# Last layer's state-space stage: squares between two silus, their addition one unit later, mask tiles behind five output products

## The chip, the cores and the metric

The kernel is one program for one core of one Trainium2 chip. It computes a whole model of four layers in one launch. The metric is the device time of an execution in microseconds (us); smaller is better. The core has a matmul engine (TensorE, PE in the profile), a vector engine (VectorE, DVE), an activation engine (ScalarE, ACT), a general engine (GpSimd, POOL) and an engine that here only starts transfers (SyncE, SP). Each takes its instructions in the order of the program; they wait for one another through semaphores.

## The reference, cut to the stage that is changed

The change is in the last layer's attention, a state-space layer of 4096 inner columns (64 heads of 64). `hidden_states` is 1024 rows of 256. What matters:

```
z   = (hidden_states @ W_in)[..., :4096]
x   = silu(causal_conv1d((hidden_states @ W_in)[..., 4096:8192], conv_w, conv_b))
dt  = softplus(dt + dt_bias);  dtx = dt * x
L   = exp(where(mask, dA_cs[i] - dA_cs[j], -inf))        # per chunk of 128 rows, per head
Y   = einsum(C, B, L, dtx);  y = Y + D * x
yg  = y * silu(z)
rms = rsqrt(mean(yg * yg, over the 4096 columns) + 1e-5)
out = (yg * rms * norm_w) @ W_out
```

The mean of squares runs over all 4096 columns, so the squares of every part of `yg` are added up, and `rms` is applied once, at the end, to the summed products.

## The kernel before

`l3_attn` cuts the 4096 columns into N = 32 units of 128 columns (one pair of heads). Unit j is one call of each engine's `pair`; the units 0 to 3 are written out, the units 4 to 31 run in a loop of two units per pass (`passes`). Columns lie on the partitions, the 1024 rows along the free dimension in two halves of 512, or eight blocks of 128. s = j % 2 chooses the buffer.

**TensorE in unit j** (line 2803 on). First the output products of unit j-3 (`output`, L2797): eight products, each `yg` block by `wo`, summed over all units into four PSUM banks. Each stands in the trace as two records of 128x256. In the midst of them stands `free_for_differences`, which waits until VectorE has read what lies in the banks 4 to 7 (semaphores xt_read and y_read); it is put right before the last product of the part that it is given. Then `differences`: sixteen small mask tiles (L2764, which write the large negative numbers of the mask) and four matmuls (L2769) that put dA_cs[i] - dA_cs[j] into the banks 4 to 7. Then the other output products. Then 24 projection matmuls (L2827), which give x and z halves; y of unit j-1 (`make_y`, L2784, 32 records), whose halves wait for ScalarE's silu of z; and the transposes of x (L2839), one group of four per half, whose halves wait for ScalarE's silu of x.

**ScalarE in unit j** (line 2922 on): four exponentials (L2913) of the differences; `squares` (L2920), which writes the squares of yg of unit j-2 into `ysq`, the one buffer of them; two evacuations of x (L2658, the first tap of the convolution); a table load (L2944); silu of z half 0 (L2950), silu of x half 0 (L2952), silu of z half 1, silu of x half 1; a table load (L2955). A silu of x waits for the convolution of its half on VectorE.

**VectorE in unit j**: `weigh` (L3032), four multiplications of 128x512 with both inputs in SBUF, called n0 to n3 below, each behind its exponential; six convolution taps (L2662), three per half, with one input in PSUM; `skip` (L3045), two; the two multiplications by dt (L3080), which free the transposes' banks and raise xt_read; `gate` (L3054), two, both inputs in SBUF.

**GpSimd in unit j**: in every other unit `steps` (L3122, L3124); the two halves of the weights' split (L3147, L3150), small copies (L3156, L3159); `scale_output` (L3136), which scales `wo` for unit j-1 and waits until the output products of unit j-3 are done; waits for its own last results and a semaphore to SyncE (L3168), upon which SyncE fetches weights; `add_squares` (L3129), 128x1024, sqsum += ysq, both inputs in SBUF, for unit j-2.

`ysq` is written by `squares` and read by `add_squares`: the squares of one unit wait (sq_added) until those of the unit before it have been added. At the end TensorE sums sqsum over the partitions (L2856), which waits for the last addition.

Of the kernel before, what the change touches and what calls it, by code (L numbers as in the profile page):

```python
# [2584 lines left out]
def l3_attn(k):  # L2585
# [11 lines left out]
    with Stage(k, "L3a", k.now) as st:  # L2597
# [81 lines left out]
        def early(j, n=2):  # L2679

            return isinstance(j, int) and j < n

        ln = Norm(k, st)
        with nc.Block() as block:
# [14 lines left out]
            def _(pe):  # L2699
# [89 lines left out]
                def output(pe, j, o, half, part=range(4), of_next=None):  # L2789

                    pe.wait_ge(S["wo_ready"], j + 1)
                    pe.wait_ge(S["y_ready"], j * 2 + half + 1)
                    for b in part:
                        g = 4 * half + b
                        if b == part[-1] and of_next is not None:
                            free_for_differences(pe, *of_next)
                        mm = nc.tensor.matmul(ps[g // 2][:, (g % 2) * C:(g % 2 + 1) * C],  # L2797
                                              yg[:, o, g * P:(g + 1) * P], wo[:, o, :], start=False, stop=False,
                                              skip_group_check=True)
                    if half == 1 and part[-1] == 3:  # L2800
                        mm.then_inc(S["out_done"], 1)

                def pair(pe, j, s, i):
                    first = is_first(j)
                    if is_second(j):
                        clear_sums(pe)
                    if not early(j, 3):
                        output(pe, j - 3, 1 - s, 0)
                        output(pe, j - 3, 1 - s, 1, (0, 1), (j, i))
                    elif not first:  # L2810
                        free_for_differences(pe, j, i)
                    if not first:
                        differences(pe, s)
                    if not early(j, 3):
                        output(pe, j - 3, 1 - s, 1, (2, 3))
                    if first:
                        make_cs(pe)
                    pe.wait_ge(S["w_split"], j + 1)
                    for at_d, (name, wm, sem) in enumerate((("x", wx[s], "x_psum"), ("z", wz[s], "z_psum"))):
                        for half in range(2):  # L2820
                            if first:
                                pe.wait_ge(S["bc_conv"], at_d + 1)
                            else:
                                pe.wait_ge(S["diff_read"], j * 4 + 2 * at_d + half + 1)
                            for kc in range(KC):
                                for at, (a, b) in enumerate(THREE):
                                    mm = nc.tensor.matmul(bank(name, half)[:, :], wm[a][:, kc, :],  # L2827
                                                          (xh, xl)[b][:, kc, half * HALF:(half + 1) * HALF],
                                                          start=(kc + at == 0), stop=(kc + at == KC + 1))
                            mm.then_inc(S[sem], 1)  # L2830
                    if first:
                        make_cb(pe)
                    else:
                        make_y(pe, j, 1 - s)
                    for half in range(2):
                        pe.wait_ge(S["x_ready"], j * 2 + half + 1)
                        for b in range(4):
                            g = 4 * half + b
                            mm = nc.tensor.transpose(bank("t", half)[:, b * P:(b + 1) * P],  # L2839
                                                     xT[:, s, g * P:(g + 1) * P], k.ident)  # L2840
                        mm.then_inc(S["xt_psum"], 1)
                    if first:
                        free_for_differences(pe, j, i)
                        differences(pe, s)
# [21 lines left out]
            def _(act):  # L2866
# [55 lines left out]
                def pair(act, j, s, i):  # L2922
                    first = is_first(j)
                    if not first:
                        exponents(act, j, s)
                    if not early(j):
                        squares(act, j - 2, s)
                    act.wait_ge(s_load[s], i * 16 + 16)
                    if first:
                        sums(0)  # L2930
                        sums(1)
                    if early(j):
                        act.wait_ge(S["bc_ready"], j + 1)
                    for half in range(2):
                        act.wait_ge(S["x_psum"], j * 2 + half + 1)
                        conv_first(act, bank("x", half)[:, :],
                                   conv[:, s, 4 * half:4 * half + 4, :].rearrange("p b t -> p (b t)"),
                                   taps[s][:, 3:4], cb[s]).then_inc(S["x_scaled"], 1)
                    if first:
                        bc_silu(1, cT)  # L2940
                        sums(2)
                        sums(3)
                    else:
                        nc.scalar.preload_act_table(ACT.Silu)  # L2944
                    for half in range(2):
                        t = slice(half * HALF, (half + 1) * HALF)
                        act.wait_ge(S["z_psum"], j * 2 + half + 1)
                        if not early(j):
                            act.wait_ge(S["y_ready"], j * 2 - 2)
                        nc.scalar.activation(sz[:, s, t], bank("z", half)[:, :], ACT.Silu).then_inc(S["z_read"], 1)  # L2950
                        act.wait_ge(S["x_conv"], j * 2 + half + 1)
                        nc.scalar.activation(xT[:, s, t],  # L2952
                                             conv[:, s, 4 * half:4 * half + 4, :].rearrange("p b t -> p (b t)"),
                                             ACT.Silu).then_inc(S["x_ready"], 1)
                    nc.scalar.preload_act_table(ACT.Exp)  # L2955
                    if first:
                        exponents(act, j, s)
# [148 lines left out]
            def _(pool):  # L3106
# [32 lines left out]
                def pair(pool, j, s, i):  # L3139

                    if not early(j) and s == 0:
                        steps(pool, i)
                    pool.wait_ge(s_load[s], i * 16 + 16)
                    if not early(j):
                        pool.wait_ge(S["z_psum"], j * 2 - 2)
                    w2 = slot[s][:, 0:2 * KC * P]
                    nc.gpsimd.tensor_tensor(wh[:, s, :], w2, k.c["zero"].to_broadcast([P, 2 * KC * P]),  # L3147
                                            ALU.add).then_inc(S["w_high"], 1)
                    pool.wait_ge(S["w_high"], j + 1)
                    nc.gpsimd.tensor_tensor(wl[:, s, :], w2, wh[:, s, :].bitcast(F32),  # L3150
                                            ALU.subtract).then_inc(S["w_split"], 1)

                    if not early(j):
                        pool.wait_ge(S["xt_read"], j * 2 - 2)
                    hs = slice(j * 2, j * 2 + 2) if isinstance(j, int) else bass.ds(j * 2, 2)
                    nc.gpsimd.tensor_copy(dtc[:, s, :, :], dt[:, :, hs]).then_inc(S["pair_small"], 1)  # L3156
                    if not early(j):
                        pool.wait_ge(S["y_read"], j * 2 - 2)
                    nc.gpsimd.tensor_tensor(dcols[:, s, :], dcol[s], k.c["zero"], ALU.add).then_inc(S["d_ready"], 1)  # L3159
                    if is_second(j):  # L3160
                        steps(pool, 0)
                    if not is_first(j):
                        scale_output(pool, j - 1, 1 - s)
                        pool.wait_ge(S["x_ready"], j * 2)
                        pool.wait_ge(S["w_split"], j)
                        pool.wait_ge(S["wo_ready"], j)
                        pool.wait_ge(S["d_ready"], j)
                        pool.sem_inc(S["slot_read"], 2)  # L3168
                    if not early(j):
                        add_squares(pool, j - 2)  # L3170

                def tail(pool):
                    scale_output(pool, N - 1, 1)
                    add_squares(pool, N - 2)
                    add_squares(pool, N - 1)

# [745 lines left out]
```

## Time and profile before

| what | value |
|---|---|
| median of 3 runs | 1874.9 us (1874.17 to 1876.9) |
| profiled execution, its own time | 1872.17 us |
| its span in the trace | 1870.0 us |
| PE busy | 1655.7 us (89%) |
| DVE busy | 1175.1 us (63%) |
| ACT busy | 931.7 us (50%) |
| POOL busy | 461.8 us (25%) |
| units 3 to 31 of the stage | about 1126 to 1527 us of the span, 13.5 or 13.7 us each |

Busy shares are averages over all stages of the model. A row of the timeline gives the start in the span, the duration in us, the engine, line and operation, the tiles written and read, and in brackets the idle time of the engine ahead of it with what ended it. For a merged row (x4) the duration runs from the first start to the last end. The modelled ends of PE records overlap with the next starts, so PE is read by its starts.

### The profile page before, as it was taken

The numbers are of one execution on the slowest core, as the hardware profiler recorded it, in microseconds if no ns is written. First come the engines' busy times: TensorE is split into PE (matmuls) and PEld (weight loads), VectorE is DVE, ScalarE is ACT, GpSimd is POOL, SyncE is SP. The second block draws the span as 40 slices with busy tenths as digits, with TensorE's granted clock in tenths as the row PEclk, the third lists the DMA queues.
The fourth block names the chain that finished last, engine by engine and source line by source line (L and its number), as shares of the span: only waits on it lengthen the run. The fifth ranks groups of instructions, "written<-read, shape, count | busy, mean of one in ns | idle before, by whom it ended". The sixth has DMA issues, their size and how long they took to land. (4 is left out here: it accounts for less than half of the span.)

```text
span 1870.0 us, 38238 instructions
## 1 busy us (share of the span) xinstructions
PE 1655.7 (89%) x14220; PEld 1276.5 (68%) x14220; DVE 1175.1 (63%) x2316; ACT 931.7 (50%) x1979; POOL 461.8 (25%) x510
## 2 busy tenths in 40 slices
PE   7988856789999889996688869999999987999898
PEld 4767733558888745663477747777777766888687
DVE  4676688556666622224665588888888875666642
ACT  2455567236656521121255456676766644555552
POOL 2030021023333131221400225454454531000220
PEclk9999978799999999998799889999999998999999
DMA  2020000300000092222000100010101003111000
GB/s 103 3 94 3 4 30 31 117 18 27 26 25 25 18 371 45 47 35 67 14 2 3 50 18 27 26 34 26 34 26 33 27 9 126 35 34 34 1 1 24
DMA packets 27684, 77.91 MB, mean 42 GB/s; under 512 B 2993, under 2 KB 14897, under 8 KB 25393
## 3 DMA queue, kind: packets, MB, share of 16 engines
q1 hardware_dynamic: 23488, 71.19, 11.1%
q0 software_dynamic: 4080, 5.13, 1.7%
q8 instruction: 79, 1.29, 0.3%
q14 instruction: 37, 0.30, 0.1%
HBM read 63.03 MB, written 13.28 MB: 41 GB/s over the span
## 5 line engine op out<-in xcount | busy, mean ns | idle before, releaser
L2662 DVE SCALAR_TENSOR_TENSOR arena<-bank,arena 128x508 f32<-128x508 f32 (+2 forms) x204 | 151.5, 743 | 18.4 <-DVE arena L2662 6.6
L3032 DVE TENSOR_TENSOR L3a_decays<-L3a_decays,L3a_cb_masked 128x512 f32<-128x512 f32 x128 | 94.8, 799 | 49.5 <-ACT L3a_decays L2913 49.5
L2797 PE MATMUL bank<-L3a_wo,L3a_y_gated 128*128 128x256 f32 x512 | 125.0, 388 | 0.0
L2913 ACT ACTIVATE L3a_decays<-bank 128x512 f32<-128x512 f32 x128 | 66.1, 604 | 103.3 <-PE bank L2769 103.3
L2827 PE MATMUL bank<-L3a_xnT_high,L3a_w_high 128*128 128x512 f32 x256 | 105.1, 410 | 1.5 <-ACT L3a_decays L2913 1.5
L2797 PEld LDWEIGHTS bank<-L3a_wo,L3a_y_gated 128*128 128x128 f32 x512 | 91.2, 190 | 21.0 <-issue 11.4
L228 PE MATMUL bank<-const 128*128 128x512 f32 (+1 forms) x154 | 73.7, 619 | 33.7 <-PEq L66 33.7
L2827 PE MATMUL bank<-L3a_xnT_high,L3a_w_low 128*128 128x512 f32 x256 | 100.5, 392 | 0.0
L2827 PE MATMUL bank<-L3a_xnT_low,L3a_w_high 128*128 128x512 f32 x256 | 100.2, 391 | 0.0
L3129 POOL TENSOR_TENSOR arena<-arena 128x1024 f32<-128x1024 f32 x32 | 86.3, 2695 | 44.4 <-ACT arena L2920 44.4
L2064 ACT ACTIVATE arena<-bank 128x512 f32<-128x512 f32 x23 | 13.7, 597 | 145.4 <-PE bank L2013 145.4
L2013 PE MATMUL bank<-L1f_experts,xnT 128*128 x184 | 85.0, 606 | 0.8 <-DVE xnT L2116 0.6
L228 PEld LDWEIGHTS bank<-const 128*128 128x128 f32 x154 | 29.2, 201 | 65.6 <-issue 65.4
L827 ACT ACTIVATE L1x_p<-bank,L1x_minus_max,L1x_q_scale 128x128 f32<-128x128 f32 x128 | 56.6, 452 | 32.0 <-DVE L1x_minus_max L1861 32.0
L2784 PE MATMUL bank<-L3a_decays,L3a_dtx 128*64 128x128 f32 x1024 | 67.2, 279 | 3.9 <-ACT arena L2950 2.1
L2784 PEld LDWEIGHTS bank<-L3a_decays,L3a_dtx 128*64 128x64 f32 x1024 | 54.8, 136 | 22.0 <-ACT arena L2950 17.9
L827 ACT ACTIVATE L3x_p<-L3x_masked_scores,L3x_minus_max 128x128 f32<-128x128 f32 x128 | 49.7, 389 | 38.8 <-DVE L3x_minus_max L3368 38.8
L2110 DVE TENSOR_TENSOR L1f_hidden<-arena,bank 128x512 f32<-128x512 f32 x23 | 15.8, 688 | 82.5 <-PE bank L2013 82.5
L1974 POOL DMA_INDIRECT rows_added<-L1f_y,L1f_token x23 | 35.7, 1554 | 114.9 <-DVE L1f_y L2129 111.8
L1689 POOL TENSOR_TENSOR L1x_q_squares<-L1x_qT 128x512 f32<-128x512 f32 x32 | 36.6, 1161 | 101.6 <-ACT L1x_qT L1802 101.6
L672 POOL TENSOR_TENSOR x<-x,arena 128x256 f32<-128x256 f32 x48 | 34.6, 756 | 109.3 <-ACT xn L215 96.4
L2952 ACT ACTIVATE L3a_xT<-arena 128x512 f32<-128x512 f32 x64 | 40.2, 628 | 37.8 <-DVEq L3070 37.8
(643 smaller groups left out, 4654.5 us busy)
## 6 DMA issues: line engine op xcount, KB each, us to landing
arena<-in_L3p SPq DMA_DIRECT2D x32, 388.0 KB, 3.0
L1f_experts<-in_L1f SPq DMA_DIRECT2D x8, 1536.0 KB, 18.9
arena<-in_L1x SPq DMA_DIRECT2D x18, 384.0 KB, 3.0
arena<-in_L3x SPq DMA_DIRECT2D x18, 384.0 KB, 3.0
arena<-in_L0f SPq DMA_DIRECT2D x1, 4224.0 KB, 12.9
arena<-in_L3f SPq DMA_DIRECT2D x1, 4055.0 KB, 12.8
rows_sent<-L1a_blank SPq DMA_DIRECT2D x1, 2967.0 KB, 13.6
xnT<-rows_sent SPq DMA_DIRECT2D x23, 129.0 KB, 2.0
```

The costliest lines, as they stand in the source:

```text
L228: self.nc.tensor.matmul(self.k.ps[bank][:, 0:width], self.k.ident, self.k.const[:, 0:width], start=True, stop=True)
L827: ins = nc.scalar.activation(self.p[:, h, b * P:(b + 1) * P], src[:, b * P:(b + 1) * P], ACT.Exp, bias=self.nb[:, h, b:b + 1], scale=scale ...
L1689: nc.gpsimd.tensor_tensor(sq[:, h * HALF:(h + 1) * HALF], q, q, ALU.mult).then_inc(s_sq, 1)
L2013: mm = nc.tensor.matmul(ps[2 * (t % 2) + m][:, :], rowsT[:, t % 2, kc, :], experts[:, bass.ds(first + (m * KC + kc) * I, I)], start=(kc == 0),
L2662: return nc.vector.scalar_tensor_tensor(dst[:, :, d:], psum[:, :, 0:P - d], wcol, dst[:, :, d:], ALU.mult, ALU.add)
L2784: mm = nc.tensor.matmul(bank("y", half)[h * HD:(h + 1) * HD, b * P:(b + 1) * P], dtx[:, o, g, h, :], dec[:, o, h, g, :], start=True, stop= ...
L2797: mm = nc.tensor.matmul(ps[g // 2][:, (g % 2) * C:(g % 2 + 1) * C], yg[:, o, g * P:(g + 1) * P], wo[:, o, :], start=False, stop=False, ski ...
L2827: mm = nc.tensor.matmul(bank(name, half)[:, :], wm[a][:, kc, :], (xh, xl)[b][:, kc, half * HALF:(half + 1) * HALF], start=(kc + at == 0), ...
L2913: nc.scalar.activation(d4[:, n * HALF:(n + 1) * HALF], bank("d", n)[:, :], ACT.Exp).then_inc(S["diff_read"], 1)
L2952: nc.scalar.activation(xT[:, s, t], conv[:, s, 4 * half:4 * half + 4, :].rearrange("p b t -> p (b t)"), ACT.Silu).then_inc(S["x_ready"], 1)
L3032: nc.vector.tensor_tensor(d, d, cbm[:, 4 * half:4 * half + 4, :].rearrange("p b t -> p (b t)"), ALU.mult).then_inc(S["dec_ready"], 1)
L3129: nc.gpsimd.tensor_tensor(sqsum, sqsum, ysq, ALU.add).then_inc(S["sq_added"], 1)
```

## The change

Three things, all in `l3_attn`. `squares(act, j - 2, s)` no longer stands behind the exponentials, but behind the silu of z half 1, ahead of the silu of x half 1. `add_squares` in unit j adds the squares of unit j-3, not j-2, and the end has three additions instead of two. The output products of TensorE are split five and three around the mask tiles and differences, where they were split six and two; the wait of `free_for_differences` moves with them and stands ahead of the fifth product.

```diff
                         output(pe, j - 3, 1 - s, 0)
-                        output(pe, j - 3, 1 - s, 1, (0, 1), (j, i))
+                        output(pe, j - 3, 1 - s, 1, (0,), (j, i))
                     if not first:
                         differences(pe, s)
                     if not early(j, 3):
-                        output(pe, j - 3, 1 - s, 1, (2, 3))
+                        output(pe, j - 3, 1 - s, 1, (1, 2, 3))
...
                         exponents(act, j, s)
-                    if not early(j):
-                        squares(act, j - 2, s)
                     act.wait_ge(s_load[s], i * 16 + 16)
...
                         nc.scalar.activation(sz[:, s, t], bank("z", half)[:, :], ACT.Silu).then_inc(S["z_read"], 1)
+                        if half == 1 and not early(j):
+                            squares(act, j - 2, s)
                         act.wait_ge(S["x_conv"], j * 2 + half + 1)
...
                         pool.sem_inc(S["slot_read"], 2)
-                    if not early(j):
-                        add_squares(pool, j - 2)
+                    if not early(j, 3):
+                        add_squares(pool, j - 3)
...
                 def tail(pool):
                     scale_output(pool, N - 1, 1)
+                    add_squares(pool, N - 3)
                     add_squares(pool, N - 2)
                     add_squares(pool, N - 1)
```

On ScalarE, in the loop's unit, from the last exponential (L2913) to the silu of x half 1 (L2952); this is the piece of the difference, in which unmarked rows stand in both kernels and lines from 2926 on are shifted:

```order
 L2913 ACTIVATE L3a_decays<-bank 128x512
+L2926 ISA
+L2933 REGISTER_ALU
+L2658 ACTIVATE arena<-bank,arena 128x512
+L2933 REGISTER_ALU
+L2658 ACTIVATE arena<-bank,arena 128x512
+L2942 ACT_TABLE_LOAD
+L2948 ACTIVATE arena<-bank 128x512
+L2952 ACTIVATE L3a_xT<-arena 128x512
+L2948 ACTIVATE arena<-bank 128x512
 L2918 ISA
 L2919 REGISTER_ALU
 L2920 ACTIVATE arena<-L3a_y_gated 128x1024
```

The squares (L2920) moved from ahead of the two evacuations (L2658) to behind the second silu of z; the number of table loads stays two per unit.

On GpSimd, in the first unit of the loop's pass, from the scaling of `wo` (L3136) on, before:

```order
L3136 TENSOR_TENSOR L3a_wo<-arena 128x256
L3129 TENSOR_TENSOR arena<-arena 128x1024
L3145 ISA
L3147 TENSOR_TENSOR L3a_w_high<-arena,const 128x512
L3149 REGISTER_ALU
L3150 TENSOR_TENSOR L3a_w_low<-arena,L3a_w_high 128x512
```

and after:

```order
L3136 TENSOR_TENSOR L3a_wo<-arena 128x256
L3128 REGISTER_ALU
L3129 TENSOR_TENSOR arena<-arena 128x1024
L3145 ISA
L3147 TENSOR_TENSOR L3a_w_high<-arena,const 128x512
L3149 REGISTER_ALU
```

The addition (L3129) keeps its place behind the scaling; what moved is the squares that it waits for: those of the unit before, not of the unit running on ScalarE.

## Rows read from the trace of the kernel before

**Rows 1.** Busy time by engine over 26 units, with granted clock (PEclk)
```profile
core 0: us, PE busy (x) PEld busy (x) DVE busy (x) ACT busy (x) POOL busy (x), PEclk, DMA share, GB/s
1150.00:1500.00 350.00, 344.65 (x2590) 261.74 (x2588) 287.91 (x414) 237.88 (x335) 173.84 (x181) 1.00 0.10 29
```
**Rows 2.** Timeline of PE, one unit; columns as told above
```profile
1308.27 0.42 PE L2764 MATMUL bank<-L3a_later_tiles,L3a_ident 32*32 32x128 bf16 x16
...
1318.56 0.66 PE L2839 MATMUL bank<-const,L3a_xT 128*128 128x128 f32 x4 [0.16 <-ACT L3a_xT L2952]
1319.05 2.77 PE L2797 MATMUL bank<-L3a_wo,L3a_y_gated 128*128 128x256 f32 x12
1321.75 0.42 PE L2764 MATMUL bank<-L3a_later_tiles,L3a_ident 32*32 32x128 bf16 x16
...
1322.54 1.13 PE L2797 MATMUL bank<-L3a_wo,L3a_y_gated 128*128 128x256 f32 x4
```
**Rows 3.** Timeline of ACT, the same unit
```profile
1311.16 1.08 ACT L2920 ACTIVATE arena<-L3a_y_gated 128x1024 f32<-128x1024 f32 x1
1312.11 1.64 ACT L2658 ACTIVATE arena<-bank,arena 128x512 f32<-128x512 f32 x2
1313.76 1.28 ACT L2944 ACT_TABLE_LOAD   x1
...
1316.07 0.59 ACT L2950 ACTIVATE arena<-bank 128x512 f32<-128x512 f32 x1
1317.87 0.63 ACT L2952 ACTIVATE L3a_xT<-arena 128x512 f32<-128x512 f32 x1 [1.21 <-DVEq L3070]
```
**Rows 4.** Timeline of DVE, the same unit
```profile
1309.86 2.92 DVE L3032 TENSOR_TENSOR L3a_decays<-L3a_decays,L3a_cb_masked 128x512 f32<-128x512 f32 x4 [1.58 <-ACT L3a_decays L2913]
1312.94 2.30 DVE L2662 SCALAR_TENSOR_TENSOR arena<-bank,arena 128x508 f32<-128x508 f32 x3 [0.16 <-ACT arena L2658]
1315.48 2.30 DVE L2662 SCALAR_TENSOR_TENSOR arena<-bank,arena 128x508 f32<-128x508 f32 x3 [0.24 <-DVE arena L2662]
...
1319.52 1.28 DVE L3080 TENSOR_TENSOR L3a_dtx<-bank,L3a_dt_pair 128x512 f32<-128x512 f32 x2
```
**Rows 5.** Timeline of POOL, the same unit
```profile
1310.27 0.76 POOL L3136 TENSOR_TENSOR L3a_wo<-arena 128x256 f32<-128x256 f32 x1 [4.12 <-PE bank L2797]
1312.32 2.73 POOL L3129 TENSOR_TENSOR arena<-arena 128x1024 f32<-128x1024 f32 x1 [1.29 <-ACT arena L2920]
```
**Rows 6.** Timeline of DVE, single records of the same unit's weighing, n1 and n3
```profile
1310.47 1.10 DVE L3032 TENSOR_TENSOR L3a_decays<-L3a_decays,L3a_cb_masked 128x512 f32<-128x512 f32 x1
1312.10 0.68 DVE L3032 TENSOR_TENSOR L3a_decays<-L3a_decays,L3a_cb_masked 128x512 f32<-128x512 f32 x1
```
**Rows 7.** Timeline of unit 1, DVE and POOL, then one undisturbed POOL record of later
```profile
1105.52 1.53 DVE L3032 TENSOR_TENSOR L3a_decays<-L3a_decays,L3a_cb_masked 128x512 f32<-128x512 f32 x1
1106.46 1.48 POOL L3147 TENSOR_TENSOR L3a_w_high<-arena,const 128x512 fp32r<-128x512 f32 x1
1106.97 1.52 DVE L3032 TENSOR_TENSOR L3a_decays<-L3a_decays,L3a_cb_masked 128x512 f32<-128x512 f32 x1
1108.02 1.43 POOL L3150 TENSOR_TENSOR L3a_w_low<-arena,L3a_w_high 128x512 fp32r<-128x512 f32 x1
...
1140.83 1.04 POOL L3147 TENSOR_TENSOR L3a_w_high<-arena,const 128x512 fp32r<-128x512 f32 x1
```
**Rows 8.** Timeline of the stage's end: POOL, DVE, POOL, PE
```profile
1526.30 0.61 POOL L3136 TENSOR_TENSOR L3a_wo<-arena 128x256 f32<-128x256 f32 x1 [7.70 <-PE bank L2797]
1526.87 2.37 POOL L3129 TENSOR_TENSOR arena<-arena 128x1024 f32<-128x1024 f32 x1
...
1528.82 0.96 DVE L3054 TENSOR_TENSOR L3a_y_gated<-L3a_y_gated,arena 128x512 f32<-128x512 f32 x1
...
1531.61 2.35 POOL L3129 TENSOR_TENSOR arena<-arena 128x1024 f32<-128x1024 f32 x1 [2.38 <-ACT arena L2920]
...
1535.05 1.84 PE L2856 MATMUL bank<-const,arena 128*128 128x1 f32 x16
```
**Rows 9.** Busy time and granted clock in four 2 us stretches, units 1 and 2
```profile
1115.00:1117.00 2.00, 0.90 (x7) 0.42 (x5) 2.00 (x4) 1.66 (x2) 0.63 (x2) 1.00 0.00 0
1117.00:1119.00 2.00, 0.87 (x20) 0.36 (x20) 1.68 (x3) 0.41 (x1) 0.12 (x1) 0.96 0.35 71
1119.00:1121.00 2.00, 1.67 (x4) 1.41 (x5) 1.78 (x3) 2.00 (x5) 0.00 (x0) 0.50 0.33 132
1121.00:1123.00 2.00, 2.00 (x7) 1.57 (x7) 0.71 (x2) 1.27 (x2) 1.33 (x1) 0.69 0.00 0
```

## What the change will do to the time

> **What bounds the kernel now.** I read the busy time by stretch first. Over 26 units of the stage PE is busy 344.65 of 350 us at full clock, VectorE 287.91 [rows 1]. So the matmul engine looks like the bound, with 2% left. The timelines of one unit say what that 2% is, and that a second bound is just as near. Let T be the start of the mask tiles (1308.27 in the unit shown). The next tiles start at 1321.75, so this unit is 13.48 us long [rows 2]. A loop through four engines closes in exactly that time: tiles, exponentials, weighing from T+1.59, first tap at T+4.67, last tap done at T+9.51, silu of x half 1 at T+9.60 [rows 3, 4], second transposes at T+10.29, for which PE waits, output products at T+10.78, and after twelve records of them (six products) the next tiles at T+13.48 [rows 2]. Twelve records take 2.70 us, one product 0.45 us. The loop shows an idle PE ahead of the second transposes; hence both what shortens this loop and what lengthens it counts.
>
> The second view is VectorE against GpSimd. The weighing takes 2.92 us [rows 4], though n3 alone is 0.68 long; n1 is 1.10 long [rows 6]. GpSimd's scaling L3136 came at 1310.27, in the midst of n0, and ended at 1311.03; n1 ended at 1311.57, 0.54 later [rows 5, 6]. In unit 1 the two engines alternate: L3147 starts at 1106.46 and lasts 1.48, where it needs 1.04 undisturbed; n2, recorded from 1106.97, ends at 1108.49, 0.55 after L3147's end; L3150, which came during that, ends at 1109.45 [rows 7]. So a multiplication of VectorE with two SBUF inputs and such an instruction of GpSimd never run side by side: whoever comes while the other runs waits for all of it, and one that has waited goes before the other's next. The disputed instruction itself shows it twice. L3129 needs 2.37 undisturbed [rows 8] but 2.73 when it came at 1312.32 while n3 was running [rows 5]: it ended at 1315.05, so it ran from 1312.68, about 0.1 before n3's recorded end of 1312.78. At the stage's end a `gate` that came under L3129 lasted 0.96 and ended 0.54 after it [rows 8]. The taps, one input in PSUM, keep 2.30 us for three under a running L3129 [rows 4, 5].
>
> **The products.** With five products ahead of the tiles, 0.45 us goes out of the loop, and three follow. PE's own work is unchanged. Everything tied to the tiles (exponentials, weighing) starts 0.45 earlier against the end of the output products, and so against L3136, which waits for them. L3136 now comes at T+2.00 [rows 2, 5]; it will come at T+2.45.
>
> **The squares.** Their place behind the exponentials costs 0.95 us of ScalarE (start to next start), but the evacuations behind them wait for PE's projections anyway: VectorE idles only 0.16 for the first [rows 3, 4]. In the new place they fill 0.95 of a 1.21 us wait: silu of z half 1 at 1316.07, squares 0.5 later, silu of x half 1 could start at 1317.52, before it is wanted at 1317.87 [rows 3]. No table load is added. So alone this costs nothing and gives back up to 0.16.
>
> **The addition, one unit later.** This is the part that decides. Now L3129 waits 1.29 us behind L3136 for the squares [rows 5], and comes at T+4.05, when only the tail of n3 is left. After the change its squares were made a unit ago, so it comes right behind L3136. Between the two stand only satisfied waits and one semaphore; where nothing stands between, the next starts as the first ends (1526.87 against 1526.30 + 0.61) [rows 8]. I take 0.25 us for them, an estimate with bounds of 0 and 0.5 worked from this row and from the 0.13 that GpSimd's small instructions keep between them.
>
> Now the order on the shared resource. n0 from T+1.59; n1 recorded from T+2.20, runs until T+2.88 and lets go at T+2.75 (0.13 before its end, since L3136 must have begun at 1310.42 to be through at 1311.03, and n0 of 0.68 would be recorded to 1310.54). L3136 comes at T+2.45, inside n1, and runs T+2.75 to T+3.36 (0.61 undisturbed [rows 8]). n2 follows, ends at T+3.90, lets go at T+3.77. L3129 comes at T+3.36 + 0.25 = T+3.61, while n2 runs, so it is next: T+3.77 to T+6.14. n3 must wait and ends 0.54 later, at T+6.68 instead of T+4.51. The taps start at T+6.61 (a follower starts 0.07 before the recorded end) instead of T+4.67: **1.94 us later**. Nothing hides it: the last tap, the silu of x half 1, the second transposes and the output products are the loop. The wait ahead of the fifth product needs L3080, which ends at T+12.53 now [rows 4] and at T+14.47 then, while the fifth product's weights would load at about T+14.4: bounds 0 and 0.3, I take 0.10. Per unit: -0.45 + 1.94 + 0.10 = **+1.59 us**.
>
> The Trainium skill, SBUF — State Buffer, section "Who interferes with whom", says that a VectorE instruction with two SBUF inputs contends with a GpSimd instruction that reads SBUF, and that the loser fully blocks; by a shared bandwidth the sum would be the third rival below, by the lock it is this one, and the traces of unit 1 agree with the lock. The skill's Perfetto Trace Analysis, section "GPSIMD Engine Instruction", warns that GpSimd's recorded spans are unreliable and start-to-start spacing should be used; by spacing, L3147 to L3150 in unit 1 is 1.56 us and the alternation stays, so the sum would stay too.
>
> **The ends.** Additions run in the units 3 to 31, 29 of them. The tiles of unit 3 come 0.45 earlier; 28 intervals follow, 28 x 1.59 = 44.5; unit 31's transposes are late by 1.94 with no tiles behind. At the end of the stage three additions stand in a row. Now the last one ends at 1533.96 and L2856 starts at 1535.05 [rows 8]. The first (2.37) frees `ysq` at about 1529.3, squares take 1.06, the second addition ends near 1532.8, squares again, the third near 1536.3: L2856 starts near 1536.4, **+1.35**. Sum: 44.5 - 0.45 + 1.94 + 1.35 = 47.3 us. The profiled execution took 1872.17 (span 1870.0); that gives 1919.5, and since its time is 2.7 under the median of 1874.9, **1922.2** for the median. Own range by per-unit bounds of 1.3 to 2.0 (the tiles' wait, and 0.2 either way for reading starts): 1914 to 1934.
>
> **Rivals.** (1) *L3129 misses n2.* If it comes more than 0.41 us behind L3136's end, n2 has let go and n3 holds on; the addition then waits and disturbs only taps, which it doesn't slow. Then the weighing ends near T+4.5, the taps start near T+4.6, and the squares in their new place bound the silu, at 9.25 of the old count (1317.52): 0.35 less per unit, 29 x 0.35 = 10.2, less 1.35 at the end: 1866.1, faster. For it: the margin is only 0.16, and GpSimd's starts are the least certain. Against it: 0.04 of overlap in rows 8, and four plain waits would have to cost over 0.1 each. (2) *Sharing.* If VectorE only ran at half pace under L3129, n3 would end near T+5.5: taps +0.78, per unit -0.45 + 0.78 + 0.05 = 0.38, 28 of them 10.6, with ends of -0.45 + 0.78 + 1.35 12.3, hence 1887.2. Rows 7 speak against. (3) *The clock.* PE will idle some 2 us per unit, 1.3 of it in one piece (silu of z half 1 stands behind silu of x half 0 on ScalarE, which waits for the late taps). After unit 1, with PE busy 0.9 of 2 us for several stretches, the granted clock fell to 0.50, the 1.2 GHz level, and 2 us went at that level [rows 9]. Were that so once in each unit, another 1 us per unit would be lost, 1950.2. Against it: between the gaps PE is busy over 5 us on end.
>
> **How the numbers follow.** Forecast 0.80, rival 1 0.12, rival 2 0.04, rival 3 0.04. The forecast's own range holds most of its 0.80 (0.76); from 1886 it takes in rival 2, up to 1945 the thinner part of rival 3: 0.81 or so. Rival 1 alone is on the faster side: faster by over 0.2% (3.7 us, about what a measurement of this kernel can tell from no change) 0.12, within it 0.01, slower 0.87.
>
> **What would show it.** In the profile after: the four L3032 of a unit together 5.1 us rather than 2.92, one of them near 2.9 (in rows 7 the longest is 1.53); L3129 starting 0.1 to 0.4 behind L3136's end, and lasting about 2.5; L3136 near 0.9; the first tap with no wait for ScalarE; PE waiting for the silu of z half 1 (L2784) and longer for the silu of x half 1 (L2839); units of 15.1 us; a mean clock of 1.00. A longest L3032 near 1.1 and L3129 behind n3 would mean rival 1; all four L3032 stretched alike would mean rival 2. What makes the prediction wrong is the one number 0.25, against its threshold of 0.41.

## The result and the profile after

| | before | after |
|---|---|---|
| median | 1874.54 us (4 runs) | 1933.29 us (4 runs, 1927.40 to 1933.57) |
| ratio | 1 | 1.0298, interval 1.0282 to 1.0314 |
| span of the profiled execution | 1870.0 us | 1931.6 us |
| mean of the 28 unit intervals from unit 3's to unit 31's tiles | 13.56 us | 15.40 us |

The change makes the kernel 3% slower. The forecast was 1922.2 in a range of 1886 to 1945. The direction and the mechanism hold; the size was 11 us short.

The row of busy times by stretch, over the same 350 us as [rows 1]: PE is idle 39.5 us of 350 where it was idle 5.4, and the granted clock is still 1.00.

```profile
1150.00:1500.00 350.00, 310.48 (x2276) 230.72 (x2276) 301.94 (x362) 215.79 (x297) 153.09 (x159) 1.00 0.09 26
```

The timeline of VectorE in one unit (T = 1304.40), the answer to [rows 4, 6]: first the weighing as a whole, then its single records n0 to n3, then the two groups of taps and L3080.

```profile
1306.00 5.13 DVE L3032 TENSOR_TENSOR L3a_decays<-L3a_decays,L3a_cb_masked 128x512 f32<-128x512 f32 x4 [1.35 <-ACT L3a_decays L2913]
...
1306.00 0.69 DVE L3032 TENSOR_TENSOR L3a_decays<-L3a_decays,L3a_cb_masked 128x512 f32<-128x512 f32 x1 [1.35 <-ACT L3a_decays L2913]
...
1306.61 0.69 DVE L3032 TENSOR_TENSOR L3a_decays<-L3a_decays,L3a_cb_masked 128x512 f32<-128x512 f32 x1
...
1307.21 1.10 DVE L3032 TENSOR_TENSOR L3a_decays<-L3a_decays,L3a_cb_masked 128x512 f32<-128x512 f32 x1
...
1308.24 2.89 DVE L3032 TENSOR_TENSOR L3a_decays<-L3a_decays,L3a_cb_masked 128x512 f32<-128x512 f32 x1
...
1311.05 2.29 DVE L2662 SCALAR_TENSOR_TENSOR arena<-bank,arena 128x508 f32<-128x508 f32 x3
1313.57 2.30 DVE L2662 SCALAR_TENSOR_TENSOR arena<-bank,arena 128x508 f32<-128x508 f32 x3 [0.24 <-DVE arena L2662]
...
1317.61 1.28 DVE L3080 TENSOR_TENSOR L3a_dtx<-bank,L3a_dt_pair 128x512 f32<-128x512 f32 x2
```

The timeline of GpSimd in the same unit, the answer to [rows 5]:

```profile
1306.84 0.92 POOL L3136 TENSOR_TENSOR L3a_wo<-arena 128x256 f32<-128x256 f32 x1 [4.32 <-PE bank L2797]
1308.08 2.49 POOL L3129 TENSOR_TENSOR arena<-arena 128x1024 f32<-128x1024 f32 x1 [0.32 <-issue]
```

Read the two together, with T = 1304.40, the start of the mask tiles. L3136 comes at 1306.84 inside n1 and ends at 1307.76. n2, kept back by it, ends at 1308.31, 0.55 later. L3129 comes at 1308.08, 0.32 behind L3136, while n2 runs. It ends at 1310.57. n3, recorded from 1308.24, ends at 1311.13, 0.56 behind L3129's end. So n3 has waited for all of the addition: 2.89 us instead of 0.68. The first tap starts at T+6.65; before it was T+4.67. In the other of the two kinds of unit in the loop L3129 comes 0.25 behind L3136, and the weighing takes 5.12.

The timeline of PE in the same unit, up to the next unit's tiles, the answer to [rows 2]:

```profile
1314.59 1.09 PE L2784 MATMUL bank<-L3a_decays,L3a_dtx 128*64 128x128 f32 x16 [1.19 <-ACT arena L2948]
1315.62 0.66 PE L2839 MATMUL bank<-const,L3a_xT 128*128 128x128 f32 x4
1316.64 0.66 PE L2839 MATMUL bank<-const,L3a_xT 128*128 128x128 f32 x4 [0.37 <-ACT L3a_xT L2952]
1317.14 1.89 PE L2797 MATMUL bank<-L3a_wo,L3a_y_gated 128*128 128x256 f32 x8
1319.25 0.69 PE L2797 MATMUL bank<-L3a_wo,L3a_y_gated 128*128 128x256 f32 x2 [0.22 <-issue]
1319.87 0.42 PE L2764 MATMUL bank<-L3a_later_tiles,L3a_ident 32*32 32x128 bf16 x16
```

The second half of y waits 1.19 us for the silu of z, the second transposes wait for the silu of x, and the fifth product (the x2 row) stands apart from the four ahead of it. L3080, which its wait is for, ends at 1318.89; the tiles start at 1319.87, 0.98 later. In the other 27 of the 28 intervals it is 0.95 or 0.96.

ScalarE, the answer to [rows 3]: the squares fill part of the wait for the convolution, and the silu of x half 1 still waits 0.48 us for VectorE behind them. The squares hold nobody up.

```profile
1314.44 1.05 ACT L2920 ACTIVATE arena<-L3a_y_gated 128x1024 f32<-128x1024 f32 x1
1315.96 0.63 ACT L2952 ACTIVATE L3a_xT<-arena 128x512 f32<-128x512 f32 x1 [0.48 <-DVEq L3070]
```

### The profile page after: what moved, and what is told of

Read it like the earlier page. It is cut to its first block and busy times, and to the rows that moved or that the text cites. A ratio compares the mean times of both kernels' runs of the same rounds, so it can differ in the third digit from the quotient of the medians.

```text
span 1931.6 us, 38263 instructions
## 1 busy us (share of the span) xinstructions
PE 1670.3 (86%) x14216; PEld 1280.0 (66%) x14220; DVE 1236.8 (64%) x2316; ACT 938.0 (49%) x1979; POOL 461.5 (24%) x510
## 5 line engine op out<-in xcount | busy, mean ns | idle before, releaser
L3032 DVE TENSOR_TENSOR L3a_decays<-L3a_decays,L3a_cb_masked 128x512 f32<-128x512 f32 x128 | 159.7, 1308 | 45.9 <-ACT L3a_decays L2913 45.9
L2797 PE MATMUL bank<-L3a_wo,L3a_y_gated 128*128 128x256 f32 x512 | 131.1, 393 | 2.8 <-issue 2.7
L2913 ACT ACTIVATE L3a_decays<-bank 128x512 f32<-128x512 f32 x128 | 66.2, 605 | 99.3 <-PE bank L2769 99.3
L3129 POOL TENSOR_TENSOR arena<-arena 128x1024 f32<-128x1024 f32 x32 | 80.3, 2508 | 10.9 <-issue 8.3
L2658 ACT ACTIVATE arena<-bank,arena 128x512 f32<-128x512 f32 x68 | 52.9, 780 | 43.5 <-PE bank L2827 43.5
L228 PEld LDWEIGHTS bank<-const 128*128 128x128 f32 x154 | 29.6, 204 | 65.2 <-issue 65.1
L2952 ACT ACTIVATE L3a_xT<-arena 128x512 f32<-128x512 f32 x64 | 40.4, 631 | 51.0 <-DVEq L3070 51.0
L3136 POOL TENSOR_TENSOR L3a_wo<-arena 128x256 f32<-128x256 f32 x32 | 28.8, 901 | 135.7 <-PE bank L2797 135.7
## 6 DMA issues: line engine op xcount, KB each, us to landing
L1f_experts<-in_L1f SPq DMA_DIRECT2D x8, 1536.0 KB, 14.3
```

What stands on the lines that cost most here:

```text
L228: self.nc.tensor.matmul(self.k.ps[bank][:, 0:width], self.k.ident, self.k.const[:, 0:width], start=True, stop=True)
L2658: return nc.scalar.activation(dst, psum, ACT.Identity, bias=bias, scale=w3)
L2913: nc.scalar.activation(d4[:, n * HALF:(n + 1) * HALF], bank("d", n)[:, :], ACT.Exp).then_inc(S["diff_read"], 1)
L2952: nc.scalar.activation(xT[:, s, t], conv[:, s, 4 * half:4 * half + 4, :].rearrange("p b t -> p (b t)"), ACT.Silu).then_inc(S["x_ready"], 1)
L3032: nc.vector.tensor_tensor(d, d, cbm[:, 4 * half:4 * half + 4, :].rearrange("p b t -> p (b t)"), ALU.mult).then_inc(S["dec_ready"], 1)
L3129: nc.gpsimd.tensor_tensor(sqsum, sqsum, ysq, ALU.add).then_inc(S["sq_added"], 1)
```

## The experiments

Each unit interval below is the mean of the 28 intervals from unit 3's to unit 31's tiles in the profiled execution. It is a better witness than the total, because stages that no experiment touches differ by up to 4 us between executions: from L2856 to the end of the span it is 335.0 us in the kernel before and 339.2 in f_wait_gate_behind. The kernels a to d were timed on one chip beside the kernel before (there 1876.49 us), i, h, f and g on another (1873.39), k and e on a third (1876.81). So kernels of different groups are compared by their ratios and unit intervals.

| kernel | unit interval | total, median | ratio to before, interval |
|---|---|---|---|
| a_wait_weigh | 13.37 | 1869.77 | 0.9967 (0.9956 to 0.9979) |
| b_six_two | 15.73 | 1941.05 | 1.0341 (1.0321 to 1.0362) |
| c_half_add | 14.29 | 1895.50 | 1.0099 (1.0075 to 1.0122) |
| d_split_only | 13.44 | 1866.94 | 0.9955 (0.9939 to 0.9972) |
| i_gate_behind | 15.07 | 1921.46 | 1.0255 (1.0225 to 1.0284) |
| h_split_gate_behind | 13.16 | 1862.34 | 0.9939 (0.9923 to 0.9955) |
| f_wait_gate_behind | 13.20 | 1865.41 | 0.9955 (0.9941 to 0.9969) |
| g_squares_only | 15.25 | 1918.60 | 1.0241 (1.0203 to 1.0279) |
| k_wait_third | 13.36 | 1869.56 | 0.9959 (0.9945 to 0.9973) |
| e_wait_six_two | 13.32 | 1868.32 | 0.9961 (0.9943 to 0.9979) |

**a_wait_weigh: the addition behind the weighing.** Against the changed kernel:

```diff
                     if not early(j, 3):
+                        pool.wait_ge(S["dec_ready"], j * 4 + 4)
                         add_squares(pool, j - 3)
```

> The changed kernel, in which GpSimd's addition L3129 also waits until VectorE's fourth multiplication n3 of the same unit is done. Nothing else is moved. Theory 1 (exclusive turns: n3 had to wait for all of L3129): n3 is 0.68 us long again, the weighing about 2.9 us, the first tap starts near T+4.6 (T = start of the mask tiles), units of 13.3 to 13.6 us, total 1868 to 1878. Rival A (the loss is from the squares between two silus delaying the silu of x half 1): the addition's place is innocent, units stay at 15.4 us, total near 1930. Rival B (the loss is from the split five and three, with its earlier wait): the same, near 1930.

One added wait takes the unit from 15.40 to 13.37 us and the total from 1933 to 1870. GpSimd's addition and the whole weighing of one unit, from this kernel's timelines:

```profile
1308.07 2.40 POOL L3129 TENSOR_TENSOR arena<-arena 128x1024 f32<-128x1024 f32 x1 [1.31 <-DVE L3a_decays L3032]
...
1305.00 2.92 DVE L3032 TENSOR_TENSOR L3a_decays<-L3a_decays,L3a_cb_masked 128x512 f32<-128x512 f32 x4 [1.35 <-ACT L3a_decays L2913]
1308.00 2.30 DVE L2662 SCALAR_TENSOR_TENSOR arena<-bank,arena 128x508 f32<-128x508 f32 x3
```

The addition lasts 2.40, near its undisturbed 2.37, beside taps that keep 2.30, and the weighing is 2.92 again. Squares and split stand as in the changed kernel, so the rivals A and B, by which one of them was the loss, are out. The order of the two engines' instructions was the loss; with that order mended, the changed kernel is no longer slower than the one before.

**c_half_add: the price against the length of the addition.** This kernel leaves half of the squares out of the sum.

```diff
-                    nc.gpsimd.tensor_tensor(sqsum, sqsum, ysq, ALU.add).then_inc(S["sq_added"], 1)
+                    nc.gpsimd.tensor_tensor(sqsum[:, 0:HALF], sqsum[:, 0:HALF], ysq[:, 0:HALF], ALU.add).then_inc(S["sq_added"], 1)
```

> The changed kernel in which every addition L3129 adds only the first 512 of 1024 columns; the other half of the squares is left out of the sum. It lasts about 1.2 us instead of 2.37. Theory 1 (n3 waits for the whole instruction): the longest L3032 falls from 2.89 to about 1.7 us, units fall from 15.41 by 1.18 to about 14.2, total 1933 - 28 x 1.18 - 2 = about 1897. Rival C (VectorE runs at a part of its pace under GpSimd): the weighing shrinks by half as much, units near 14.8, total near 1915.

The unit falls by 1.11 us to 14.29, the total to 1895.5. In this kernel's timelines n3 is 1.77 long, ends at 1306.30, and the addition ends at 1305.75:

```profile
1304.31 1.44 POOL L3129 TENSOR_TENSOR arena<-arena 128x512 f32<-128x512 f32 x1 [0.26 <-issue]
...
1304.53 1.77 DVE L3032 TENSOR_TENSOR L3a_decays<-L3a_decays,L3a_cb_masked 128x512 f32<-128x512 f32 x1
```

n3 ends 0.55 or 0.56 behind the addition whether that is long or short. So it waits for the whole instruction; sharing at a part of the pace (rival C, 1915) would have halved the difference.

**k_wait_third: who comes first.** As a_wait_weigh, with j * 4 + 3 in place of j * 4 + 4.

> The changed kernel, in which the addition waits for VectorE's third multiplication n2, not for the fourth. Theory 1 (whoever comes first has the turn, and for all of it): the semaphore of n2 lets L3129 come about 0.1 us after n2's end, when n3, recorded from 0.07 before n2's end, has already begun; so n3 stays 0.68 long, L3129 waits for it (2.7 us long), and the units are the 13.37 us of the kernel that waits for n3; total 1866 to 1874. This also tests the forecast's threshold: 0.41 us after L3136's end. Rival (GpSimd always wins, or the two share): n3 is lengthened by 1 to 2.4 us and the total is 1895 to 1933.

The addition now comes at 1309.15 behind n2. n3 has been recorded from 1308.92, keeps its 0.68, and the addition is the one that waits (2.72 instead of 2.40):

```profile
1309.15 2.72 POOL L3129 TENSOR_TENSOR arena<-arena 128x1024 f32<-128x1024 f32 x1 [0.71 <-DVE L3a_decays L3032]
...
1308.92 0.68 DVE L3032 TENSOR_TENSOR L3a_decays<-L3a_decays,L3a_cb_masked 128x512 f32<-128x512 f32 x1
```

L3136 ends at 1308.45 here, so the addition came 0.70 behind it. In the changed kernel it came 0.32 behind it and in this case cost 2 us a unit. The threshold of 0.41 lies between the two; it was not approached closer.

**b_six_two: the changed kernel with the old split.**

```diff
-                        output(pe, j - 3, 1 - s, 1, (0,), (j, i))
+                        output(pe, j - 3, 1 - s, 1, (0, 1), (j, i))
...
-                        output(pe, j - 3, 1 - s, 1, (1, 2, 3))
+                        output(pe, j - 3, 1 - s, 1, (2, 3))
```

> The changed kernel with the output products split six and two again, as before; squares and additions stay as changed. Theory 1: L3136 now comes in n0, L3129 in n1, so n2 (not n3) waits for all of L3129 and lasts near 2.9 us; the weighing ends near T+6.7 all the same, the wait ahead of the sixth product costs nothing, and units take 13.56 + 1.94 = 15.5 us: total 1925 to 1935. Rival B (the split is the cause): back to about 1875.

The split is not the cause: without it the kernel is slower still, by a ratio of 1.0341 where the changed kernel has 1.0298. It is also 6 us above the 1925 to 1935 that were expected. Here it is n2 that lasts 2.89, as expected, since L3136 and L3129 come one multiplication earlier. Most units take 15.44 to 15.66, where 15.5 was expected, but 6 of 28 take 16.45. Busy times over one unit that stays short (the first two rows) and one that doesn't (the other three) show what differs; the columns are those of [rows 1]:

```profile
1298.00:1301.00 3.00, 1.30 (x19) 0.89 (x18) 2.66 (x5) 1.39 (x4) 2.92 (x3) 1.00 0.00 0
1301.00:1303.00 2.00, 1.65 (x20) 1.24 (x20) 1.62 (x3) 1.51 (x3) 0.28 (x2) 1.00 0.00 0
...
1313.50:1316.50 3.00, 1.38 (x18) 0.85 (x16) 2.66 (x5) 1.39 (x4) 1.74 (x3) 1.00 0.00 0
1316.50:1318.50 2.00, 1.92 (x17) 1.59 (x18) 1.55 (x3) 1.52 (x3) 0.00 (x0) 0.56 0.00 0
1318.50:1320.50 2.00, 2.00 (x10) 1.97 (x11) 1.94 (x4) 1.36 (x2) 0.19 (x1) 0.59 0.00 0
```

PE has been idle for 1.63 us between the two halves of y, and then the granted clock falls to the 1.2 GHz level for some 3 us. Six such units, each 0.8 to 1.0 us longer, make up about the 6 us above what was expected (an estimate from the intervals). This is rival 3 of the prediction. But a gap of that length doesn't decide it alone: the unit of the first two rows has a gap of 1.64 us, every one of the 28 has one of 1.62 us or more, and the clock falls in only six. In the changed kernel, with gaps of 1.2, the clock stayed at 1.00 over the 350 us above.

**d_split_only: the split alone, on the kernel before.** The diff is the reverse of the one above.

> The kernel before, with only the output products split five and three; squares and additions as before. Theory 1 with the wait ahead of the fifth product costing 0.10 us, as predicted: L3129 still comes at T+4.05 behind n2, units shorter by 0.45 - 0.10, but no less than PE's own work of about 13.1, total near 1865. With that wait costing 0.40 us, as the changed kernel's trace suggests: units shorter by 0.05 only, total 1872 to 1876. In both the weighing stays at 2.9 us.

13.44 us a unit, 1866.9 in all: 0.45% faster than before. The gain of 0.12 us a unit lies between the two expectations. In all 28 intervals the tiles follow 0.95 to 0.99 behind L3080's end, here from 1315.05 to 1316.01:

```profile
1313.77 1.28 DVE L3080 TENSOR_TENSOR L3a_dtx<-bank,L3a_dt_pair 128x512 f32<-128x512 f32 x2
...
1316.01 0.42 PE L2764 MATMUL bank<-L3a_later_tiles,L3a_ident 32*32 32x128 bf16 x16
```

So part of the split's 0.45 us is lost to the wait ahead of the fifth product, here too.

**i_gate_behind: the waits for the banks behind the fifth product.** The changed kernel with:

```diff
                     for b in part:
                         g = 4 * half + b
-                        if b == part[-1] and of_next is not None:
-                            free_for_differences(pe, *of_next)
                         mm = nc.tensor.matmul(...)
+                    if of_next is not None:
+                        free_for_differences(pe, *of_next)
+                        pe.sem_inc(S["tiles_free"], 1)
```

(`tiles_free` is a new semaphore that nobody waits for; it only stands between the waits and the mask tile.)

> The changed kernel, with TensorE's waits for the banks (free_for_differences) put behind the fifth output product instead of ahead of it. Theory 1, with the part of the prediction that was too small named: in the changed kernel the tiles start 0.97 us behind the end of L3080 in every unit, because the fifth product starts only after the wait; the loop closes over L3080 and not over the second transposes. With the wait behind the product the tiles start at T + 12.74 + 2.25 = T+15.0 to 15.1, units 15.4 -> 15.05, total about 10 us under the changed kernel's 1933: 1920 to 1926. The weighing stays at 5.1 us. Rival (the extra 11 us over the forecast are from elsewhere, such as the clock): units stay at 15.4, total 1930 to 1934.

1921.46 us, 15.07 a unit. The products now run through, ten records in 2.26 us, and the tiles start with 0.51 behind L3080's end (1314.40 to 1314.91) instead of 0.98:

```profile
1312.65 2.32 PE L2795 MATMUL bank<-L3a_wo,L3a_y_gated 128*128 128x256 f32 x10
1314.91 0.42 PE L2764 MATMUL bank<-L3a_later_tiles,L3a_ident 32*32 32x128 bf16 x16
```

**h_split_gate_behind: the kernel before, split and waits moved, nothing else.** d_split_only with the diff of i_gate_behind.

> The kernel before, with the products split five and three and the waits for the banks behind the fifth product. Theory 1: without this the split alone gives units of 13.45 us with the tiles 0.96 behind the end of L3080; now the tiles start when the fifth product is through, output products at T+10.85, tiles at T+13.1: units 13.1 to 13.25 us, which is TensorE's own work; total about 28 x 0.27 = 8 us under the split alone's 1867: 1857 to 1863. Rival: TensorE's work bounds at 13.45 already: no change against the split alone.

13.16 us a unit, 1862.34 in all, 0.61% faster than before: the shortest unit and the lowest time of the kernels tried, though its interval overlaps with those of f, d, k and e. PE is busy 338.27 of 340 us, so little but PE's own work is left in the stage:

```profile
1150.00:1490.00 340.00, 338.27 (x2592) 264.96 (x2591) 288.64 (x414) 239.11 (x337) 177.48 (x182) 1.00 0.09 29
```

**f_wait_gate_behind: all of the change, both amendments.** a_wait_weigh with the diff of i_gate_behind.

> The changed kernel with both amendments: the addition waits for the fourth multiplication, and the waits for the banks stand behind the fifth product. Theory 1: units from 13.37 to 13.1 or 13.2 us, total 1862 to 1866, 1 to 3 us over the same without moved squares, for the three additions in a row at the stage's end cost 1.5 us or so.

13.20 us, 1865.41. The changed kernel can be had 0.45% faster than before with the two amendments, but h_split_gate_behind, which leaves squares and additions alone, is no slower. From the last tiles to L2856 the three additions in a row cost 1.5 us (24.8 against 23.3).

**g_squares_only: the squares alone, the addition left behind them in the same unit.** The ScalarE part of the change's diff on the kernel before.

> The kernel before, with only the squares moved between the two silus; the addition stays in the same unit and so waits for them. Theory 1: the squares cost ScalarE nothing, but the addition runs near T+9.4 to T+11.8, and GpSimd's queue behind it (steps, weights' split) is then late for TensorE in every second unit by 0.5 to 1.3 us: total 1882 to 1897. Rival (squares in that place delay the silu of x half 1 itself): ScalarE's row of the silu starts later than its convolution is done, in every unit.

Expected up to 1897, measured 1918.6: the direction was right, the price was too small. Units alternate between 14.7 and 15.9. The rival accounts for very little: ScalarE's silu of x half 1 starts at 1310.01, 0.24 behind the end of its taps (1309.77), where it was 0.09 in the kernel before (1317.78 to 1317.87), so the squares hold it by 0.15 us at most. GpSimd's queue is the first part of the loss. The addition waits for the squares until 1323.67; behind it stand the next unit's steps, the last of which ends at 1328.77, and the sixth output product waits for them:

```profile
1323.67 2.36 POOL L3129 TENSOR_TENSOR arena<-arena 128x1024 f32<-128x1024 f32 x1 [5.66 <-ACT arena L2920]
1326.54 0.78 POOL L3122 TENSOR_TENSOR L3a_diff_left<-L3a_cs_left,const 128x256 fp32r<-128x256 f32 x1 [0.50 <-POOL arena L3129]
1327.29 1.48 POOL L3124 TENSOR_TENSOR L3a_diff_right<-xn,const 128x512 fp32r<-128x512 f32 x1
...
1329.19 0.69 PE L2797 MATMUL bank<-L3a_wo,L3a_y_gated 128*128 128x256 f32 x2 [2.02 <-POOL L3a_diff_right L3124]
```

L3124 itself is 1.48 here instead of 1.04, because it now meets VectorE's `gate`.

The second part of the loss is the clock. Behind that gap of 2 us ahead of the sixth product the granted clock falls to the 1.2 GHz level:

```profile
1295.50:1298.50 3.00, 1.04 (x5) 0.57 (x3) 1.73 (x3) 0.00 (x0) 2.59 (x3) 1.00 0.00 0
1298.50:1302.50 4.00, 3.94 (x27) 2.55 (x28) 1.46 (x3) 2.07 (x4) 2.12 (x5) 0.64 0.00 0
```

There are 14 such gaps in the loop, one in every second unit, and the clock falls behind 13 of them, all but the first. The unit behind the first takes 13.21 us, those behind the others 14.61 to 14.76. So the clock costs about 13 x 1.48 = 19 us (an estimate from these intervals), most of the 21.6 us by which the time lies above the upper end of what was expected.

With the squares in their new place the addition must therefore move too, if it isn't to hold up the steps behind it, and where it moves to was the question of this case.

**e_wait_six_two: squares and addition moved, the addition behind the weighing, the old split.**

> The changed kernel with the addition behind the fourth multiplication, as before, and the output products split six and two again: only the squares' new place and the later addition are left of the change. Theory 1: the first tap no longer waits 0.16 us for ScalarE, the loop over the second transposes shortens by that, units 13.40 instead of 13.57, the three additions at the end cost 1.35 us: total 1870 to 1874 against 1874 before. Rival (squares in front of the silu of x half 1 delay it): units of 13.6 or more, total 1875 to 1880.

13.32 us a unit, 0.24 less than before, and 1868.3 in all. The first tap follows the weighing without the 0.16 us wait; with T = 1302.93 it starts at T+4.43, where it was T+4.67:

```profile
1304.52 2.92 DVE L3032 TENSOR_TENSOR L3a_decays<-L3a_decays,L3a_cb_masked 128x512 f32<-128x512 f32 x4 [1.59 <-ACT L3a_decays L2913]
1307.36 2.29 DVE L2662 SCALAR_TENSOR_TENSOR arena<-bank,arena 128x508 f32<-128x508 f32 x3
```

So the squares' new place is worth a little, as the prediction said, and somewhat more than its 0.16, since a follower also starts 0.07 to 0.08 ahead of the recorded end. The rival is out.

## Why the prediction was right, and what was too small

**What bounds the kernel.** Right. The loop through tiles, weighing, taps, silu, transposes and output products exists, and both ways of shortening it (d_split_only, e_wait_six_two) shorten the unit.

**The order on the shared resource.** Right, within 0.07 us. Foretold: L3136 at T+2.45, n2's end T+3.90, L3129 at T+3.61, n3's end T+6.68, first tap T+6.61. Measured: T+2.44, T+3.91, T+3.68, T+6.73, T+6.65. The number on which all hung, L3129's distance behind L3136's end, was 0.32 in this kind of unit and 0.25 in the other, under the 0.41 of the threshold. It had been an estimate with bounds of 0 and 0.5, which reach beyond the threshold, so that it fell on the foretold side was in part luck. c_half_add and k_wait_third show the rule apart from this kernel's timing.

**The squares cost nothing by themselves.** Right as to ScalarE (the silu of x half 1 still waits for the convolution behind them), and e_wait_six_two has the gain. But "alone this costs nothing" holds only of ScalarE: with the addition left in the same unit, g_squares_only is 2.4% slower.

**The wait ahead of the fifth product: 0.10 us a unit, bounds 0 and 0.3.** This is the term that was mis-sized, and its measured value lies just outside its bounds. Over the 28 intervals the unit grew by 15.40 - 13.56 = 1.84 instead of 1.59. I had added the wait to the way over the second transposes, as a delay of a weight load. That is 0.35 for the term, if the 1.94 is kept; the first tap itself came 1.98 later instead of 1.94, which leaves 0.31. The trace shows another way that closes the loop: taps, L3045, L3080, the wait, then the fifth product, then the tiles. L3080 ends at T+14.49, as foretold (T+14.47); but the tiles start 0.98 after that, T+15.47, since the product itself, 0.45, and its start stand behind the wait. Taken as a second path it would have been in reach: [rows 2, 4] have 0.95 between L3080's end and the tiles already, and that or 0.96 is the least distance in the kernel before, met in every second unit. i_gate_behind takes this path away and saves 0.33 us a unit: 15.07, where the forecast without its 0.10 gives 13.56 - 0.45 + 1.94 = 15.05. That its total, 1921.46, is near the forecast of 1922.2 is partly chance, as the next sum shows.

**The sum.** The span grew by 61.6 us:

| | foretold | measured |
|---|---|---|
| ahead of unit 1's tiles | 0 | 2.2 |
| unit 1's tiles to unit 3's | -0.45 | 0.74 |
| 28 unit intervals | 44.5 | 51.7 |
| last tiles to L2856 | 3.3 | 3.5 |
| from L2856 on | 0 | 3.5 |
| sum | 47.3 | 61.6 |

Of the 14.3 us that were missing, 7.2 are the mis-sized term. The three additions at the end came out as worked. Nearly all of the rest, 6.9, is of a size that also stands between executions of kernels that do the same work there. The 2.2 ahead of unit 1 are there at the first normalisation already (row below: L155 starts at 247.1; before 245.1, and in h_split_gate_behind, which is faster, 246.9), so they are a difference between executions, not the change's:

```profile
L155 DVE BATCH_NORM_AGGREGATE ln_mv<-ln_stats x16: 123/150/182, 247.1 to 1604.8; 128x2 f32<-128x6 f32 x16
```

From unit 1's tiles to unit 3's it is 1.2 us more than foretold. In unit 2 the projections ran at the lower clock for 6.8 us in the execution after; before, it was 3.4 us [rows 9]. The gap in front of them is in both. The kernels a_wait_weigh and k_wait_third have the same instructions up to unit 3; from unit 1's tiles to unit 3's the one took 28.4 us and the other 29.6, with a granted clock of 0.88 and 0.76 over 1114 to 1128 us, as before and after have. So this too is a difference between executions. Soon behind the stage, over 10 us, the granted clock was 0.67 (the last row):

```profile
1123.00:1125.00 2.00, 2.00 (x6) 1.60 (x5) 1.77 (x2) 0.47 (x1) 1.92 (x2) 0.50 0.00 0
1125.00:1127.00 2.00, 2.00 (x6) 1.52 (x5) 1.59 (x3) 0.31 (x1) 0.87 (x2) 0.50 0.00 0
...
1604.10:1614.10 10.00, 7.70 (x32) 6.42 (x33) 6.70 (x22) 6.20 (x11) 5.03 (x4) 0.67 0.89 339
```

The 3.5 us from L2856 on need not be the change's either. a_wait_weigh has the same three additions and the same 1.35 us of idle PE ahead of L2856, and takes 335.6 us from there to the end; before it is 335.0, after 338.5, and 338.3 in h_split_gate_behind, which leaves squares and additions alone.

**The rivals.** Rival 1 (L3129 misses n2) is false in this kernel and true in k_wait_third. There the first tap starts at T+4.6, as foretold, but the unit is 13.36 us and not 13.56 - 0.35 = 13.21: the tiles again stand 0.95 to 0.98 behind L3080's end, the path that the forecast left out. Rival 2 (sharing) is false; the prediction once calls it the third rival below, where it stands second. Rival 3 (the clock) didn't occur in the changed kernel's loop but does in b_six_two and g_squares_only.

## What to carry to other kernels

An instruction that is "off the critical path" and gets its inputs earlier also starts earlier, and what it then runs beside can cost more than the wait that was removed: list, for each engine that shares something, what it does in the stretch into which the work falls. When such a collision is found, a wait that holds back the instruction whose result nobody waits for can be enough (here one line, 63 us). And when an instruction stands behind a wait that isn't its own, as the fifth product does here, its own duration is in the path of what the wait is for: look for the last instruction that the wait waits for, and count from its end.

## What the runs showed of the hardware

The exclusive turns of VectorE and GpSimd were expected from unit 1's rows. New is how sharply the order of arrival decides: 0.32 us behind the other's end costs VectorE 2.2 us on a 0.68 us instruction, 0.70 us costs it nothing and GpSimd 0.3. Unexpected too was how near the clock is: idle gaps of PE of 1.2 us per unit left it at the 2.4 GHz level in 28 units of 15.4 us; gaps of 1.6 us or a little more in each of 28 units (b_six_two) cost it for some 3 us in six of them; gaps of 2.0 us in every second unit (g_squares_only) cost it behind 13 of 14. Why it fell behind some gaps of b_six_two and not behind others of the same length is left open here.
